# Scaling the listed sums of a graph network on ScalarE, block by block, instead of on VectorE, four blocks at a time

## The reference

```python
def _edge_conv(x, src, dst, edge_attr, W, b, denom):
    msg = jnp.concatenate([x[src], edge_attr], axis=1) @ W + b
    s = jax.ops.segment_sum(msg, dst, num_segments=x.shape[0])
    return s / denom[:, None]
counts = jax.ops.segment_sum(jnp.ones((src.shape[0],)), dst, num_segments=x.shape[0])
denom = jnp.maximum(counts, 1.0)
h = _edge_conv(x, src, dst, edge_attr, W0, b0, denom)
outputs = [h]
for W, b in ((W1, b1), (W2, b2), (W3, b3)):
    cat = jnp.concatenate(outputs, axis=1)
    outputs.append(_edge_conv(cat, src, dst, edge_attr, W, b, denom))
return _layernorm(x + outputs[-1])
```

## Time and profile before

| | us |
|---|---|
| median of 3 runs | 1001.54 (1001.44 to 1001.55) |
| the profiled execution | 1003.43 |
| its span, first to last instruction | 1001.6 |
| busy in the span: POOL | 703.4 |
| VectorE | 685.1 |
| ScalarE | 513.0 |
| TensorE matmuls | 461.7 |
| update 1: POOL's first and last accumulating DMA start | 565.53, 615.19 |
| update 2: the same | 671.91, 721.39 |

### The profile page before, as it was taken

One profiled execution on the slowest core, in us unless ns is written; L12 is line 12 of the kernel. 1 busy time (PEld: TensorE's weight loads), 2 busy tenths in 40 slices (PEclk: granted clock), 3 DMA queues, 4 the chain that ended last, 5 costly groups with the idle time before them and its releaser, 6 DMA issues.

```text
span 1001.6 us, 13461 instructions
## 1 busy us (share of the span) xinstructions
PE 461.7 (46%) x2876; PEld 344.1 (34%) x2876; DVE 685.1 (68%) x2422; ACT 513.0 (51%) x1350; POOL 703.4 (70%) x652
## 2 busy tenths in 40 slices
PE   2456655777757889977925200540045561000000
PEld 1346553554534556644514200430045551000000
DVE  6888898877866987676566667848669973798000
ACT  7667774756546667665614066425565540276100
POOL 6677776777752777777757387738777873777775
PEclk9555565656557999999858555755557875555555
DMA  6899993999994577655577299948999981654111
GB/s 176 232 292 273 292 305 88 314 327 315 294 371 158 198 245 239 222 193 202 200 227 242 52 269 312 335 125 213 298 344 327 320 274 50 199 162 144 53 50 38
DMA packets 224327, 224.65 MB, mean 224 GB/s; under 512 B 18994, under 2 KB 206251, under 8 KB 224207
## 3 DMA queue, kind: packets, MB, share of 16 engines
q1 hardware_dynamic: 193551, 153.22, 49.1%
q0 software_dynamic: 26336, 44.55, 16.5%
q10 hardware_dynamic: 4320, 25.56, 6.2%
HBM read 116.84 MB, written 132.35 MB: 249 GB/s over the span
## 4 chain that ended last, share of the span: by engine, by line
POOL 16%; DVE 12%; DMA 10%; issue 8%; PE 5%; ACT 2%; DVEq 0%; POOLq 0%; SPq 0%
POOL out_rows L739 6%; POOL part_rows L713 4%; POOL G L700 4%; DVE AC L1642 3%; DMA area<-x_and_z_of_nodes 3%; PE segp L2109 2%; POOL EC L732 2%; DMA G<-part_rows,dsti 2%; DMA G<-part_rows,previ 1%; DMA G<-part_rows,s0r 1%; DVE area L1657 1%; DMA EC<-x_and_z_of_nodes,idx 1%; ACT area L880 1%; DMA out_rows<-area 1%; PE hp L2109 1%
## 5 line engine op out<-in xcount | busy, mean ns | idle before, releaser
L666 POOL DMA_INDIRECT G<-x_in,srci x196 | 210.1, 1072 | 78.5 <-issue 54.5
L676 POOL DMA_INDIRECT x_and_z_of_nodes<-area,sum_rows x140 | 141.4, 1010 | 66.7 <-ACT area L852 36.9
L880 ACT ACTIVATE area<-area,AC 128x128 f32<-128x128 f32 x299 | 117.5, 480 | 43.1 <-DVE AC L1664 43.1
L700 POOL DMA_INDIRECT G<-part_rows,s0r x70 | 78.2, 1118 | 23.6 <-issue 18.6
L818 ACT ACTIVATE UT<-segp,UT 128x1 f32 x168 | 43.9, 261 | 96.5 <-PE segp L1868 72.3
L852 ACT ACTIVATE area<-hp,zero,inv 128x512 f32<-128x512 f32 x72 | 53.3, 775 | 63.5 <-DMA x_and_z_of_nodes<-area,sum_rows 28.7
L2103 PE MATMUL segp<-ZERO 128*128 128x390 f16 (+1 forms) x34 | 14.2, 419 | 150.8 <-DVE EC L1684 143.1
L732 POOL DMA_INDIRECT EC<-x_and_z_of_nodes,idx x58 | 61.8, 1066 | 31.2 <-issue 16.2
L1868 PE MATMUL segp<-SX,G 128*128 128x128 f32 x336 | 80.1, 428 | 3.3 <-ACT SX L794 3.3
L1868 PEld LDWEIGHTS segp<-SX,G 128*128 128x128 f32 x336 | 73.0, 326 | 3.5 <-ACT SX L794 3.5
L873 ACT ACTIVATE AC<-AC,eps 128x13 f32<-128x13 f32 x30 | 9.2, 306 | 126.4 <-DVE AC L1650 122.7
(11 more groups left out here) (471 smaller groups left out, 1527.3 us busy)
## 6 DMA issues: line engine op xcount, KB each, us to landing
part_rows<-area SPq DMA_DIRECT2D x36, 768.0 KB, 4.3
area<-x_and_z_of_nodes SPq DMA_DIRECT2D x30, 832.0 KB, 7.8
x_and_z_of_nodes<-ZERO SPq DMA_DIRECT2D x24, 1024.0 KB
x_and_z_of_nodes<-x_in SPq DMA_DIRECT2D x24, 1024.0 KB
area<-x_in SPq DMA_DIRECT2D x23, 832.0 KB, 8.0
out_rows<-area ACTq DMA_DIRECT2D x23, 832.0 KB, 5.6
part_rows<-ZERO SPq DMA_DIRECT2D x14, 768.0 KB, 10.6
LATE<-x_in SPq DMA_DIRECT2D x7, 832.0 KB, 7.4
```

Source lines behind the costliest of these rows:

```text
L666: g.indirect_dma_start(G[:, slot, 0:D], None, x, bass.IndirectOffsetOnAxis(ap=srci[:, c:c + 1].bitcast(u32), axis=0), bounds_check=last_no ...
L676: g.indirect_dma_start(XZ2, bass.IndirectOffsetOnAxis(ap=sum_rows[:, c:c + 1], axis=0), HS3[:, q % 2, j, 3 * D:4 * D], None, bounds_check= ...
L700: g.indirect_dma_start(G[:, n % GS, 0:D], None, TB3, bass.IndirectOffsetOnAxis(ap=take[k][:, n:n + 1], axis=0), bounds_check=last_part, oo ...
L880: last = a.activation(XLS[b][:, k], XLS[b][:, k], ACT.Identity, bias=shift[:, b, r:r + 1], scale=rs[:, b, r:r + 1])
```

## The change

VectorE no longer scales. `scale_rows` moves to ScalarE's list: for each block, one activation of 128 x 128 (Identity, with the block's column of `inv_l2` as the scale) that signals `scaled[k]`. It stands ahead of the square root of chunk 2 for k = 1 and of chunk 11 for k = 2, and waits for `at_ready`, which VectorE now raises twice: after the row numbers, and after round 2. POOL waits for `scaled[k]` ahead of every block's DMA. VectorE goes from the end of round k to the seven chunks. ScalarE reads the number of units of the update once more at the start of this half.

```diff
--- before.py
+++ after.py
@@ -49,7 +49,6 @@
 OHG = 6
 PAYS = 2
 W1 = D + PAYS
-MB = 4
 LROUND = (None, 2, 2, 8)
 LSTAGE = (None, 7, 7)
 LLAST = 4
@@ -708,8 +707,7 @@
                 e.sem_inc(s["pool_tick"], 1)
                 def unit(u):
                     for b in range(MUNITS[u], MUNITS[u + 1]):
-                        if b % MB == 0:
-                            e.wait_ge(scaled[k], b // MB + 1)
+                        e.wait_ge(scaled[k], b + 1)
                         g.indirect_dma_start(TB3, bass.IndirectOffsetOnAxis(ap=l2_at[k - 1][:, b:b + 1], axis=0), own_row(b, w), None,
                                              bounds_check=last_part, oob_is_err=False, compute_op=ALU.add).then_inc(s["updated"], 16)
                 unit(0)
@@ -865,7 +863,7 @@
                     e.wait_ge(s["lows_turned"], 1)
                     a.copy(srct[:, :], XB[0:T // 2, 0:2 * P]).then_inc(s["lows_copied"], 1)
             nested(e, n_s, SLOTS, CIT, step)
-            n_l, = list_counts(e, (UNITS_L,))
+            n_l, n_m = list_counts(e, (UNITS_L, UNITS_M))
 
             def sqrt_rows(c):
                 b = c % RING
@@ -882,8 +880,21 @@
                 e.wait_ge(s["act_normed"], c + 1)
                 e.dma_start(ov[c], XLS[b]).then_inc(st_o[b], 16)
 
+            def scale_rows(k):
+
+                e.wait_ge(s["at_ready"], k)
+                w = W1 if k == 1 else D
+                def unit(u):
+                    for b in range(MUNITS[u], MUNITS[u + 1]):
+                        own = own_row(b, w)
+                        a.activation(own, own, ACT.Identity, bias=zero1[:, 0:1], scale=inv_l2[:, b:b + 1]).then_inc(scaled[k], 1)
+                unit(0)
+                nested(e, n_m, 1, NU, unit)
+
             REST_AT = SBASE[1] + 2
             for c in range(LCH - LLAST):
+                if c in SBASE:
+                    scale_rows(SBASE.index(c))
                 sqrt_rows(c)
                 norm_rows(c)
                 if c == REST_AT:
@@ -1745,14 +1756,7 @@
                 lnk(v.reciprocal(rs_l[q, 0, 0:1], sd_l[q, 0, 0:1]))
                 v.tensor_scalar(RX[q, 0, :], RX[q, 0, :], dev_l[q, 0, 0, 0:1], rs_l[q, 0, 0:1], ALU.subtract, ALU.mult).then_inc(s["rest_done"], 1)
 
-            def scale_rows(k):
-                w = W1 if k == 1 else D
-                def unit(u):
-                    for b in range(MUNITS[u], MUNITS[u + 1], MB):
-                        own = own_rows(b, MB, w)
-                        v.tensor_tensor(own, own, inv_l2[:, b:b + MB].unsqueeze(2).to_broadcast([P, MB, D]), ALU.mult).then_inc(scaled[k], 1)
-                unit(0)
-                nested(e, n_m, 1, NU, unit)
+            def update_chunks(k):
                 for c in range(LSTAGE[k]):
                     chunk(SBASE[k] + c)
                     if k == 1 and c == 2:
@@ -1809,9 +1813,10 @@
             for k in (1, 2):
                 link(v.tensor_scalar(l2_at[k - 1][:, :].bitcast(i32), wlo[:, 0:T], 3.0, float(k), ALU.mult, ALU.add))
             e.sem_inc(s["at_ready"], 1)
-            scale_rows(1)
+            update_chunks(1)
             round_(2, n_s2, n_g2)
-            scale_rows(2)
+            e.sem_inc(s["at_ready"], 1)
+            update_chunks(2)
             round_(3, n_e, n_g)
             link(v.memset(node_u[:, T:CT].bitcast(i32), 60000))
             link(v.tensor_tensor(wlo[:, 0:T], own_pay(0), valid1[:, 0:T], ALU.mult))
```

## The result

The changed kernel took 1005.65 us (median of 20 runs, 998.29 to 1015.8), the kernel before 1001.54 (20 runs on the same chip): ratio 1.004, 95% interval 1.0022 to 1.0058. It is slower, by about 4 us. The forecast was 1001.5, its range 997.7 to 1005.0; the time is outside it.

What follows compares the result with a forecast made beforehand. POOL's back-to-back DMAs and gathers were taken as the bound, not VectorE's chunks. Terms 0 (start), +0.4 (later adds), 0 (waits, ScalarE's queue), -1 (round 2), +0.5 (round 3) gave -0.1 us: 1001.5 us, range 997.7 to 1005.0.

Steps and rivals of the forecast that it cites:

- What bounds the kernel: Updates to round 3: POOL never waits for VectorE's chunks except at the seams between stages; gaps of 0.30 us.
- part 4: Seams behind the updates, and round 3: -1 us at round 2's end, +0.5 us for round 3's adds.
- the end of round 2: Round 2's last landing: earlier loads partly clear out of its way, -1 us, bounds +2 and -5.1.
- round 3's adds: Round 3: eight more VectorE adds among POOL's gathers, at new places, cost +0.5 us, bounds -3 and +4.
- the list of signs: Signs from update 1 to round 3, including first DMA 0.15 us earlier and round 2's first gather near 619.3.
- rival (b): Ends of rounds 2 and 3: loads clear the landings, -3 us, 998.5 us; chance 0.16.
- Part 1: First DMA of each update: POOL starts 0.15 us earlier; ScalarE's blocks take 9.4 us, none late, waits cost nothing.
- Part 2: Updates: VectorE's adds meet POOL's DMAs; 0 at the start with part 1, +0.4 us later, bounds -4 and +4.
- The -0.3 us: Both updates: sum if adds did not hold up DMA issue, keeping only part 1's gain; the forecast rejected it.
- Rival (c): Updates: adds fall badly on POOL's port need, 15 us and not 12, 3 us lost, 1004.5 us; chance 0.20.
- Part 3: ScalarE's queue in the updates: square root behind the scaling hidden by 1 us; a branch stall costs POOL nothing.
- Rival (a): Updates: chunks set the end, 3.6 us come through, 997.9 us, or 999.7 with the branch stall; chance 0.10.

Runs made afterwards that it cites:

- the hold: Changed kernel, with SP holding the loads of chunks 9 and 18 until POOL has seen the update's DMAs land: 996.97 us, ratio 0.9971 to the kernel before.
- The run with the old timing: Changed kernel plus five idle 512-wide VectorE multiplies ahead of the chunks in each update, about what the scaling took: 1002.13 us, ratio 1.0016.
- The cut add: Kernel before, with VectorE's 1664-wide add of each chunk cut into four adds of 384 or 416 columns: 994.35 us, ratio 0.9933.

## Why the prediction was wrong

**What bounds the kernel** was right: POOL runs gapless at 0.30 us inside the stages, and the chain of waits of the kernel after goes from the first DMA of update 1 to the end of round 3 through POOL's DMAs, their landings and what has to be done with them at the seams, with no layernorm chunk in it.

**The step that failed is part 4, the seams behind.** It went through the end of round 2 (-1 us) and round 3's adds (+0.5), and passed over the seam between an update and the next round. That landing stood in the rows with 2.5 us and was taken as unchanged without a reason; the sum has no term for it, though the list of signs has one, the first gather of round 2 within 1 us of 619.3. It came at 623.25. The forecast had all that was needed for it: chunks 3.6 us earlier, their loads with them, loads of z that take 6.4 and 12.5 us, and a DMA share of 0.88. It even used them, but only with the sign of a gain: "some clear out of this landing's way" (part 4, and rival (b)). For the landings behind the updates the same step brings loads into the way: +5.3 and +4.3 us. That this, and not the rest, is the slowdown is shown by the hold: 996.97 with the loads held and all else left. The run with the old timing, 1002.13, agrees.

**Part 1** held. The timeline of the kernel after at the start of update 1, all engines:

```profile
560.17 0.52 DVE L1810 TENSOR_TENSOR nhi<-UT,rela 128x196 f32<-128x196 f32 x1 [2.70 <-issue]
...
562.32 9.34 ACT L890 ACTIVATE UT<-UT,zero,nhi 128x128 f32<-128x128 f32 x24 [13.70 <-DVEq L1815]
562.38 1.89 DVE L1668 TENSOR_TENSOR area<-area 128x1664 f32<-128x1664 f32 x1
563.11 2.66 POOL L711 DMA_INDIRECT part_rows<-UT,nlo  x1 [11.80 <-ACT UT L890]
...
567.64 1.88 DVE L1668 TENSOR_TENSOR LATE<-LATE,area 128x1664 f32<-128x1664 f32 x1
...
567.95 3.00 POOL L711 DMA_INDIRECT part_rows<-UT,nlo  x1 [0.30 <-ACT UT L890]
...
571.57 0.29 ACT L871 ACTIVATE AC<-AC,eps 128x13 f32<-128x13 f32 x1
...
572.90 0.23 DVE L1674 RECIPROCAL AC<-AC 128x13 f32<-128x13 f32 x1
```

From the row numbers' first instruction to POOL's first DMA it is 2.94 us, before 565.53 - 562.35 = 3.18: 0.24 earlier, forecast 0.15. ScalarE's 24 blocks took 9.34 us, forecast 9.4. No DMA waited for a later block, and the single signals cost nothing: the gaps in the update are all 0.30 or 0.31.

**Part 2** held in kind and sum. The first DMA took 2.66 us, 1.11 over 1.55; the forecast had 0.95. Behind it six more are lengthened by over 0.5 us in update 1, the first of them the third DMA (567.95, with the add of 567.64), and five in update 2; the forecast had six in each. The excess of all 24 is 45.24 - 37.2 = 8.0 and 43.51 - 37.4 = 6.1 us, for 7.0 and 6.6 before: +0.5 together, forecast 0 for the start and +0.4. The cut add shows that most of the excess is the adds': some 60% of it goes when the add is in four (13.6 us to 5.2 in the two updates). The Trainium skill, "SBUF — State Buffer", section "Who interferes with whom", infers that a tensor_tensor does not hold up descriptor generation. The issue of the indirect DMAs here is held up by one all the same: 1000.9 us (median of 29 runs of before beside it) become 994.4 for nothing but shorter adds. (The -0.3 us that the prediction gives for that inference is the share of the two updates alone; with its own -1 for round 2, and no cost of adds in round 3, the sum would be -1.3.) Rival (c), the adds falling badly, named the right side and nearly the right time (1004.5) by the wrong mechanism: the updates lost 0.5 us, not 3.

**Part 3** held. The square root of chunk 2 follows at 571.57, at the end of the scaling (562.32 + 9.34 = 571.66; it begins 0.09 us ahead of it, by which the blocks overlap as well, 0.48 us long and 0.39 apart); it is done at 571.86 and VectorE uses it at 572.90, so it was hidden by 1.0 us, as forecast. No branch stall shows on ScalarE, though VectorE still has its 2.70 us of "issue" at the end of the round. The rule of the Trainium skill weighed there ("Runtime: NRT & Kernel Launch", "Instruction fetch mechanics") did not show at this branch.

**Part 4, the end of round 2**, had the right sign and was too small: 13.75 us before, 10.01 after. In the six kernels in which VectorE goes straight on with chunks it is 9.9 to 12.0, in before and the two kernels with its timing 13.3 to 13.8 (with the cut add alone it is 11.6, so chunks are not all that sets it): some 2 to 4 us where 1 was forecast, inside the bound of 5.1. The landing that the -1 was meant for did shorten by 1.05 us (7.75 to 6.70, the gather of 653.43), so rival (b) was right in that part. Much of the rest goes with TensorE's granted clock over the last two groups: 3.8 us for both in the three kernels with 13.3 to 13.8, 3.2 to 3.6 in the four with 11.5 to 12.0, 2.1 to 2.2 in the three with 9.9 to 10.0. Whether the earlier chunks bring the higher clock isn't shown. In the profile with both holds this seam is 2.3 us shorter than before's, as much as the whole stretch from round 1 to round 3 gains there. **Round 3** lost 2.6 us in this profile (80.8 for 78.2 us of gathers), forecast +0.5; in the other five kernels with the change and whole adds the gathers take 78.1 to 79.7, so the size is not settled by one profile.

**Rival (a)**, that chunks set the end, was wrong for the changed kernel, whose chain has no chunk until round 3 is over. The kernel with both holds comes to 997, near its 997.9; in its chain the held z of chunk 18 and the chunks behind it stand from 718.07 to about 760 and POOL's gathers behind them, so the nearness proves nothing for either. What remains open: whether x or z of the pair does the harm, by which part of the path (queue, engine or memory), what stores add to it in the kernels with the cut add, and what made the one landing of 4.12 us.

## What to carry to other kernels

When work moves forward in time, list every wait for a landing behind it and ask of each which large loads will now be issued shortly ahead of its last small DMA or beside it; a load that used to come just behind the wait is the one to look for. A gain in an engine's time can be kept by holding that load until the landing was seen, which cost nothing that could be told here (ratio 1.0012, 0.9993 to 1.003). And where the DMA issues of one engine lengthen under another's long instruction, cut that instruction: four pieces alone brought the kernel before to 994.35 us.

## What the runs showed of the hardware

- A small accumulating DMA near two loads of 832 KB keeps POOL waiting 5.0 to 7.9 us from the end of its issue instead of 2.1 to 3.1 (once 4.1), when the load of z was issued from 7.1 us ahead to 1.2 us behind its start; with loads 2.4 us behind it the wait was 2.5 to 2.6.
- An indirect DMA's issue on POOL waits for the end of the 128x1664 add that VectorE is running: 3.02 us over a whole add. With the add in four pieces it mostly waits for the piece it met only (1.76 us), but in four of some 20 cases for the last one (3.12 us at 584.40).
- ScalarE went from the end of a run-time branch to its next instruction without a gap (571.57), where VectorE stands 2.5 to 2.7 us at the end of such loops.
